# A mixture of 32 experts: fixed first blocks, paired weight loads asked for ahead, and places found before the shared expert

## The chip, the cores and the metric

The kernel runs on one core of a Trainium2 chip, as one program for a decoder of four layers. The metric is the time of one execution on the device in microseconds (us); the profiler takes one execution, and its span runs from the first to the last instruction.

## The reference, cut to what matters

Each of four layers adds a self-attention, a cross-attention and a feed-forward part to x (1024 tokens of 128 numbers). The change concerns the feed-forward part of the first layer, a mixture of experts with one choice per token and one expert that all tokens share:

```python
# H = 128, I = 256, E = 32; 1024 tokens
x = hidden_states.reshape(-1, h)
shared_out = _swiglu(x, shared_gate_w, shared_up_w, shared_down_w)
logits = x @ gate_w
topk_ids = jnp.argmax(logits, axis=-1)
topk_val = jnp.max(logits, axis=-1)
xs = x * jax.nn.sigmoid(topk_val)[:, None]
tokens_per_expert = jnp.zeros((E,), jnp.int32).at[topk_ids].add(1)
order = jnp.argsort(topk_ids)
g = ragged_dot(xs[order], routed_gate_w, tokens_per_expert)
u = ragged_dot(xs[order], routed_up_w, tokens_per_expert)
d = ragged_dot(silu(g) * u, routed_down_w, tokens_per_expert)
return shared_out + d[argsort(order)]     # _swiglu: silu(x @ gw) * (x @ uw) @ dw
```

The input of the mixture is the layer norm of x, and its result is added to x. The expert weights are one array of 33 entries, `packed`, entry 0 the shared expert, of 128 x 768 numbers each (384 KB).

## The kernel before

The program is written by engine: for each of SyncE (SP), GpSimd (POOL), VectorE, ScalarE and TensorE there is one stream of instructions that goes through the twelve parts of the decoder in order. Semaphores, wrapped in `Count` objects made by `counter`, order them: `sem.at(use, n)` is the value that a counter has after n events in its use number `use`. A stream runs strictly in its order, so an instruction that waits holds up all that stand behind it on its engine. SyncE issues nearly all transfers, on one queue.

**The first mixture (m = 0)** sorts the tokens by expert into 39 blocks of 128 rows (`blocks[0]` = 8 + 31, enough for any distribution), in `scr_x` in memory, which is filled with zero rows before. VectorE's `choose_vector` finds each token's expert. TensorE's ranking product (L1715) counts, for each token, the tokens of each expert up to it. `place_vector` finds from that how many blocks each expert needs, which expert block b belongs to (`expert_of`, event `placed` 1) and each token's row (`place`, event `placed` 2). POOL then writes the 1024 scaled tokens to their rows with eight scatters (L2044). `map_vector` turns rows back to tokens, for the way home.

The shared expert runs on TensorE between these steps: `shared_up_tensor` four times, `shared_down_tensor` once, with VectorE's multiplications `shared_vector` 0 and 1 ahead of `place_vector` and 2 and 3 behind it.

**The blocks** run in `tensor`, `scalar` and `vector`, in a loop over b from 0 to 38. Tokens come in groups of four blocks (`gb` = 4): `x_sync(g)` on SyncE loads group g from `scr_x` (256 KB, L1642) into a ring of eight blocks, and `turn_tensor(g)` transposes it on TensorE (L1783). For each block, `up_tensor` makes the two first products (L1797 and L1799, four matmuls that the trace shows as eight), ScalarE and VectorE make silu(g) * u, and `down_tensor` the second product (L1810). POOL scatters the block's result to `scr_y` (L2055). TensorE's loop is

```python
for b in range(self.nb):
    g = b // self.gb
    if b == 0:
        self.turn_tensor(pe, 0)
    if b % self.gb == self.gb // 2 and g + 1 < self.ng:
        self.turn_tensor(pe, g + 1)
    self.up_tensor(pe, b)
    if b:
        self.down_tensor(pe, b - 1)
```

so group g + 1 is turned ahead of block 4 g + 2. The weights of a block come into a ring of five slots (`WS`, `wslot`) in SyncE's `sync`: for each b from b = 4 on it waits until the last user of the slot (block b - 5; at b = 4 the shared expert) has made its second product, reads the block's expert into a register (`value_load`, L1669) and issues the load (L1670); at b = 0 it waits for the scatters and issues the token loads of groups 0 and 1, and at every b divisible by four after that the load of group b / 4 + 1.

**Before the mixture** stands the cross-attention (part n = 1). Its SyncE stream `maxima_sync` goes through 16 groups g of scores; from g = 12 on it also asks for inputs that later parts need (`late_inputs`), at the end of g = 15 it waits for them (L869) and writes the zero rows to `scr_x` and `scr_h`. The scores read the buffers `qs` (its lower half) and `ks`; the event `b_mm` counts the scores. After it, VectorE makes masks from the late inputs (L3255).

Of the kernel before, what the change touches and what calls it, by code (L numbers as in the profile page):

```python
# [79 lines left out]
def program(nc, a, ctx):  # L80
# [272 lines left out]
    class Attention:  # L353
# [497 lines left out]
        def maxima_sync(self, sp):  # L851
# [3 lines left out]
            for g in range(G):  # L855
# [11 lines left out]
                if self.n == 1 and g == G - 1:  # L867
                    sp.wait_ge(loaded, LOADED)
                    sp.dma_start(scr_x.rearrange("(p k) d -> p (k d)", p=P), w[:, 0:SLOTS]).then_inc(written, 16)  # L869
                    sp.dma_start(scr_h[0:1, :], w[0:1, 0:D]).then_inc(written, 16)  # L870
# [690 lines left out]
    m3 = range(3)  # L1561
    sh = [4 * m["shared"] for m in MOES]
# [6 lines left out]
    h_spill = counter("h_spill", [0, 4, 0], 16)  # L1569
# [8 lines left out]
    loads = [[(n + m["shared"] + WS - 1 - i) // WS for n, m in zip(blocks, MOES)] for i in range(WS)]  # L1578
    kept = [2 * len([g for g in range(LG - PR, LG) if g % 3 == i]) for i in range(WS)]
    w_in = [counter(f"w_in{i}", [n[0], n[1] + more, n[2]], 16) for i, (n, more) in enumerate(zip(loads, kept))]  # L1580
    scr_kv = nc.dram_tensor("scr_kv", [PR // 2, P, 4 * S2], F32, kind="Internal").ap()
# [21 lines left out]
    class Mixture:  # L1603
# [17 lines left out]
        def weights(self, r):  # L1621

            w, n = wslot[r % WS], self.width
            if self.relu:
                return w[:, 0:n], None, w[:, n:2 * n], w[:, 2 * n:2 * n + self.c]
            return w[:, 0:n], w[:, n:2 * n], w[:, 2 * n:3 * n], None

# [21 lines left out]
        def sync(self, sp):  # L1649
# [14 lines left out]
            sp.wait_ge(placed.sem, placed.at(m, 1))  # L1664
            for b in range(self.nb):
                r = b + self.shared
                if r >= WS:
                    sp.wait_ge(down_mm.sem, down_mm.at(m, self.sh // 2 + b - WS + 1))
                expert = sp.value_load(expert_of[b:b + 1, 0:1], min_val=0, max_val=self.e - 1 + self.shared)  # L1669
                sp.dma_start(wslot[r % WS][:, 0:n], self.packed[bass.ds(expert, 1), :, :].rearrange("o p n -> p (o n)")  # L1670
                             ).then_inc(w_in[r % WS].sem, 16)
                if self.sorted:
                    if b == self.early:
                        sp.wait_ge(sorted_out.sem, sorted_out.at(m, self.choices * NT))
                        self.x_sync(sp, 0)
                    if b == self.early or b > self.early and b % self.gb == 0 and b // self.gb + 1 < self.ng:
                        self.x_sync(sp, b // self.gb + 1)
# [72 lines left out]
        def shared_up_tensor(self, pe, k):  # L1750

            m = self.m
            gate, up, _, _ = self.weights(0)
            c, cols = k % 2, hT[:, k // 2 * 512:k // 2 * 512 + 512]
            if k >= 2:
                pe.wait_ge(hid_sb.sem, hid_sb.at(m, k - 1))
            pe.matmul(bank(k % 2), gate[:, c * P:(c + 1) * P], cols, start=True, stop=True)
            pe.matmul(bank(2 + k % 2), up[:, c * P:(c + 1) * P], cols, start=True, stop=True).then_inc(up_mm.sem, 1)

        def shared_down_tensor(self, pe):  # L1760
            m = self.m
            last = self.weights(0)[2]
# [23 lines left out]
        def up_tensor(self, pe, b):  # L1786
            m, k = self.m, self.sh + b
            r = b + self.shared
            gate, up, _, _ = self.weights(r)
            pe.wait_ge(w_in[r % WS].sem, w_in[r % WS].at(m, r // WS + 1))  # L1790
# [11 lines left out]
        def down_tensor(self, pe, b):  # L1802
            m, last = self.m, self.weights(b + self.shared)[2]
# [18 lines left out]
        def scalar(self, act):  # L1822
# [16 lines left out]
            for b in range(self.nb):  # L1839
# [6 lines left out]
                if self.relu:  # L1846
                    if b >= 2:
                        act.wait_ge(down_mm.sem, down_mm.at(m, self.sh // 2 + b - 1))
                    bias = self.weights(b + self.shared)[3]
# [44 lines left out]
        def place_vector(self, dve):  # L1894
# [6 lines left out]
            if self.choices == 1:  # L1901
# [8 lines left out]
            do(dve.tensor_scalar(need, need, ROUND, ROUND, ALU.add, ALU.subtract))  # L1910
            do(dve.memset(ones, 1.0))
# [5 lines left out]
            do(dve.scalar_tensor_tensor(out=L, in0=off.unsqueeze(1).to_broadcast([P, NT, e]), scalar=float(P),  # L1917
                                        in1=bank(6, 0, NT * 32).rearrange("p (t e) -> p t e", e=32)[:, :, 0:e],
                                        op0=ALU.mult, op1=ALU.add))
# [62 lines left out]
        def vector(self, dve):  # L1982
            m = self.m
            self.choose_vector(dve)
            if self.shared:
                self.shared_vector(dve, 0)
                self.shared_vector(dve, 1)
            self.place_vector(dve)
            xf = x[:, :, :].rearrange("p t d -> p (t d)")
            if self.shared:  # L1990
                self.shared_vector(dve, 2)
                self.shared_vector(dve, 3)
                dve.wait_ge(down_mm.sem, down_mm.at(m, 2))
                dve.tensor_tensor(xf, xf, ps[:, 4:6, :].rearrange("p b n -> p (b n)"), ALU.add).then_inc(mixed.sem, 1)
                self.map_vector(dve)
# [79 lines left out]
    g_ctx = counter("g_ctx", [1], 16)  # L2075
# [16 lines left out]
    class Gathered:  # L2092
# [23 lines left out]
        def context_tensor(self, pe):  # L2116
            pe.wait_ge(g_ctx.sem, 16)
# [134 lines left out]
    l_in = counter("l_in", [2], 16)  # L2252
# [20 lines left out]
    class Linear:  # L2273
# [141 lines left out]
        def vector(self, dve):  # L2415
            do = lambda ins: link(dve, dchain, ins)
            dve.wait_ge(l_in.sem, l_in.at(0, 2))
# [89 lines left out]
    c_in = counter("c_in", [6], 16)  # L2507
# [14 lines left out]
    class Latents:  # L2522
# [81 lines left out]
        def tensor(self, pe):  # L2604
# [6 lines left out]
            pe.wait_ge(c_in.sem, c_in.at(0, 6))  # L2611
# [85 lines left out]
        def early_turn_tensor(self, pe):  # L2697
# [5 lines left out]
            pe.wait_ge(c_in.sem, c_in.at(0, 6))  # L2703
# [109 lines left out]
        def context_vector(self, dve, half, step):  # L2813
# [3 lines left out]
            if step == 0:  # L2817
                dve.wait_ge(c_in.sem, c_in.at(0, 6))
# [84 lines left out]
    f_in = counter("f_in", [2], 16)  # L2903
# [9 lines left out]
    class Ternary:  # L2913
# [123 lines left out]
        def weights_vector(self, dve):  # L3037

            dve.wait_ge(f_in.sem, f_in.at(0, 2))
# [144 lines left out]
    def _(sp):  # L3184
# [10 lines left out]
        for s in range(N_SUB_RUN):  # L3195
            if s in subs:
                if not subs[s].prev:
                    subs[s].stack_sync(sp)
                subs[s].maxima_sync(sp)
            elif s in mixtures:  # L3200
# [272 lines left out]
```

## Time and profile before

| | before |
|---|---|
| time, median of 3 runs | 1403.6 us |
| the runs | 1397.66, 1403.6 and 3434.42 us |
| span of the profiled execution | 1397.9 us |
| TensorE busy | 1154.4 us, 83% of the span |
| VectorE busy | 888.4 us, 64% |
| ScalarE busy | 712.3 us, 51% |
| GpSimd busy | 273.4 us, 20% |
| moved by DMA | 122.46 MB, 88 GB/s on average |
| granted TensorE clock | 0.908 of full speed on average |

The profile tells the span of its own execution alone, so that the span stands for its time. The shares are averages over twelve parts with different limits, and what a change in one part does is read from the rows of that part.

### The profile page before, as it was taken

The numbers are of one execution on the slowest core, as the hardware profiler recorded it, in microseconds if no ns is written. First come the engines' busy times: TensorE is split into PE (matmuls) and PEld (weight loads), VectorE is DVE, ScalarE is ACT, GpSimd is POOL, SyncE is SP. The second block draws the span as 40 slices with busy tenths as digits, with TensorE's granted clock in tenths as the row PEclk, the third lists the DMA queues.
The fourth block names the chain that finished last, engine by engine and source line by source line (L and its number), as shares of the span: only waits on it lengthen the run. The fifth ranks groups of instructions, "written<-read, shape, count | busy, mean of one in ns | idle before, by whom it ended". The sixth has DMA issues, their size and how long they took to land.

```text
span 1397.9 us, 26573 instructions
## 1 busy us (share of the span) xinstructions
PE 1154.4 (83%) x9407; PEld 715.2 (51%) x9412; DVE 888.4 (64%) x2331; ACT 712.3 (51%) x1456; POOL 273.4 (20%) x558
## 2 busy tenths in 40 slices
PE   4889997686596399768999999999953968989994
PEld 2334344684243299555666666666643942333332
DVE  5767984334577444686676766777751166777866
ACT  3665883222452022514665665676731625656674
POOL 2522221453010256200000000000004414212220
PEclk9788999898798699989999999999985977999998
DMA  7431243684602467400000000011124825221200
GB/s 183 99 72 42 67 130 124 216 287 145 155 2 98 153 232 250 156 1 1 1 1 1 1 1 1 1 39 46 39 60 134 304 89 134 58 54 52 54 9 15
DMA packets 91620, 122.46 MB, mean 88 GB/s; under 512 B 11329, under 2 KB 69390, under 8 KB 90510
## 3 DMA queue, kind: packets, MB, share of 16 engines
q1 hardware_dynamic: 87266, 112.11, 26.4%
q0 software_dynamic: 4224, 8.66, 1.9%
q8 instruction: 77, 1.26, 0.4%
q14 instruction: 53, 0.43, 0.1%
HBM read 89.73 MB, written 30.02 MB: 86 GB/s over the span
## 4 chain that ended last, share of the span: by engine, by line
PE 62%; DVE 13%; DMA 8%; issue 5%; ACT 5%; POOL 3%; SPq 3%; DVEq 0%; ACTq 0%; POOLq 0%
PE ps L2644 7%; PE ps L2651 7%; PE ps L1168 7%; PE ps L2659 6%; PE ps L918 4%; PE ps L1797 3%; PE ps L927 3%; PE ps L1810 3%; PE ps L2733 2%; PE ps L2740 2%; PE ps L1080 2%; DMA wring<-in_L_ffn_w 2%; PE ps L1799 2%; PE ps L1203 2%; POOL scr_x L2044 2%
## 5 line engine op out<-in xcount | busy, mean ns | idle before, releaser
L1168 PE MATMUL ps<-probs,vaug 128*32 128x256 f32 (+1 forms) x1792 | 145.8, 401 | 12.4 <-ACT probs L1132 8.0
L2851 DVE CUSTOM_DVE_ANT_0 wring<-ps,probs 128x768 f32<-128x768 f32 x128 | 122.6, 958 | 46.2 <-PE ps L2644 45.5
L2810 ACT COPY qs<-ps 128x768 f32<-128x768 f32 x128 | 102.3, 800 | 90.4 <-PE ps L2651 90.4
L1123 ACT ACTIVATE probs<-ps 128x512 f32<-128x512 f32 x192 | 104.2, 595 | 62.6 <-PE ps L968 62.4
L273 POOL TENSOR_TENSOR rstd<-veps,mhalf 128x4 f32<-128x4 f32 (+2 forms) x28 | 26.5, 948 | 536.2 <-DVE veps L241 501.0
L1000 DVE TENSOR_REDUCE mx<-ps 128x2 f32<-128x1024 f32 (+1 forms) x96 | 115.5, 1220 | 20.2 <-PE ps L918 19.5
L1127 ACT ACTIVATE probs<-ps 128x512 f32<-128x512 f32 x192 | 104.8, 594 | 40.6 <-PE ps L1080 39.5
L2791 ACT ACTIVATE wring<-wring,r 128x768 f32<-128x768 f32 x128 | 120.8, 944 | 3.9 <-DVE r L2854 3.9
L2651 PE MATMUL ps<-ident,wring 128*128 128x128 f32 x768 | 110.2, 280 | 3.3 <-DVE wring L2895 3.2
L2651 PEld LDWEIGHTS ps<-ident,wring 128*128 128x128 f32 x768 | 83.4, 141 | 41.9 <-issue 35.3
L2055 POOL DMA_INDIRECT scr_y<-probs x85 | 82.1, 966 | 98.6 <-DVE probs L2009 93.3
L2644 PE MATMUL ps<-probs 64*128 64x512 f32 (+1 forms) x512 | 100.5, 511 | 1.1 <-DVE r L2851 1.1
L988 DVE CUSTOM_DVE_ANT_0 wring<-ps,m3x 128x512 f32<-128x512 f32 x128 | 83.2, 688 | 15.8 <-PE ps L918 8.7
L2659 PE MATMUL ps<-qs,ks 128*64 128x256 f32 x768 | 90.0, 384 | 0.0
L918 PE MATMUL ps<-ks,qs 49*128 49x256 bf16 (+1 forms) x512 | 81.0, 354 | 10.1 <-DMA ks<-scr_first 4.2
L2002 DVE TENSOR_TENSOR probs<-gated,ps 128x256 f32<-128x256 f32 (+1 forms) x62 | 32.2, 520 | 88.6 <-ACT gated L1857 46.8
L1797 PE MATMUL ps<-probs,wring 128*128 128x128 f32 x428 | 79.7, 293 | 8.1 <-DMA wring<-in_L_ffn_w 5.9
L2895 DVE TENSOR_SCALAR wring<-wring,r 128x768 f32<-128x768 f32 x128 | 79.5, 621 | 4.5
L1857 ACT ACTIVATE gated<-ps 128x256 f32<-128x256 f32 (+1 forms) x62 | 28.7, 463 | 87.4 <-PE ps L1799 87.4
L1797 PEld LDWEIGHTS ps<-probs,wring 128*128 128x128 f32 x428 | 63.8, 202 | 13.1 <-DMA wring<-in_L_ffn_w 9.7
L2644 PEld LDWEIGHTS ps<-probs 64*128 64x128 f32 x512 | 44.6, 187 | 47.5 <-issue 40.9
L1168 PEld LDWEIGHTS ps<-probs,vaug 128*32 128x32 f32 x1792 | 37.2, 110 | 60.8 <-issue 56.7
(366 smaller groups left out, 2337.7 us busy)
## 6 DMA issues: line engine op xcount, KB each, us to landing
wring<-in_L_ffn_w SPq DMA_DIRECT2D x19, 768.0 KB, 6.7
wring<-in_L_ffn_w SPq DMA_DIRECT2D x32, 384.0 KB, 4.2
wring<-in_L_ffn_w SPq DMA_DIRECT2D x19, 514.0 KB, 5.1
probs<-scr_x SPq DMA_DIRECT2D x14, 256.0 KB, 4.3
qs<-scr_q SPq DMA_DIRECT2D x18, 192.0 KB
qs<-scr_qx SPq DMA_DIRECT2D x16, 192.0 KB
probs<-in_L_ffn_w SPq DMA_DIRECT2D x8, 384.0 KB
probs<-in_L_ffn_w SPq DMA_DIRECT2D x4, 768.0 KB
```

The lines of the kernel that those rows point to most:

```text
L918: ins = pe.matmul(bank(at[r], i * self.keys, (i + 1) * self.keys), self.qv(s, c, r, ROWS_A, t * P, (t + 1) * P), self.kv(s, c, r, ROWS_A), ...
L1000: dve.tensor_reduce(out, src, AX.X, ALU.max, negate=True).then_inc(a_max.sem, 1)
L1123: act.activation(probs[:, s % 2, 2 * c + r, kt0 * S:(kt0 + 2) * S], bank(self.banks(3, k)[r]), ACT.Exp).then_inc(p_exp.sem, 1)
L1127: act.activation(probs[:, s % 2, 2 * c + r, kt0 * S:(kt0 + 2) * S], bank(4 + k % 2), ACT.Exp).then_inc(p_exp.sem, 1)
L1168: ins = pe.matmul(ps[32 * j:32 * j + 32, self.av_bank(s), q0:S], vaug[:, s % 2, kt, j, :], probs[:, s % 2, j, at:at + S - q0], start=(kt = ...
L1797: ins = pe.matmul(bank(k % 2)[:, at], gate[:, at], cols, start=True, stop=True)
L2644: ins = pe.matmul(bank(2 * j + lo // 512, 0, hi - lo), self.qT[rows, g % 2, k * P:(k + 1) * P], self.kT[rows, g % 3, lo:hi], start=True, s ...
L2651: ins = pe.transpose(self.buffer("turn", i, t * P, t * P + P), self.sc[:, i % 4, t * P:(t + 1) * P], ident[:, :])
L2659: ins = pe.matmul(self.buffer("sum", i, 0, S)[HW * j:HW * j + HW, :], self.v[:, i % 3, t, j * HW:(j + 1) * HW], self.pT[:, i % 2, j, t, :] ...
L2791: act.activation(self.sc[:, i % 4, :], self.sc[:, i % 4, :], ACT.Exp, bias=self.neg[:, i % 4:i % 4 + 1], accum_out=self.tot[:, i % 4:i % 4 ...
L2810: act.copy(self.pT[:, g % 2, j, :, k * P:(k + 1) * P], self.buffer("turn", i, 0, KV).rearrange("p (t n) -> p t n", n=P)).then_inc(self.out ...
L2851: dve.tensor_tensor_reduce(self.sc[:, s, :], src, self.maskb[:, u // (2 * PR), :], 1.0, -3.0e38, ALU.add, ALU.max, self.top[:, s:s + 1]).t ...
```

## The change

Block e, for e from 0 to 31, holds the first 128 tokens of expert e, whatever the others get; the seven blocks 32 to 38 hold what experts have over 128 tokens. `place_vector` therefore subtracts one block from each expert's need, finds the experts of the seven extra blocks alone, and computes a token's block from whether its rank is over 128 (three new instructions and a changed one, beside the subtraction).

The weights of blocks 0 to 31 are then known without any register: they are loaded in pairs, two experts (768 KB) in one transfer, into ten lanes (`lanes`): one slot of the ring, and parts of `qs` and `ks`. Lanes 0 to 2 are asked for by the cross-attention's SyncE stream at g = 15 after `late_inputs`, lanes 3 to 9 after its end, behind a wait for the last scores (`ahead_sync`). The others are asked for in `first_sync`, which takes the place of the loop in `sync` for this mixture. The extra blocks' weights come one by one, with the register.

On VectorE, `place_vector` follows `choose_vector` at once, then all four `shared_vector`, then `map_vector`, and then the addition of the shared expert's result to x. The lanes use counters that belonged to single later parts (`g_ctx`, `l_in`, `c_in`, `f_in`, `h_spill`); those parts count in use 1 now. The two other mixtures keep their loops.

```diff
@@ maxima_sync
                 if self.n == 1 and g == G - 1:
+                    for p in range(3):
+                        mixtures[2].lane_sync(sp, p)
                     sp.wait_ge(loaded, LOADED)
                     sp.dma_start(scr_x.rearrange("(p k) d -> p (k d)", p=P), w[:, 0:SLOTS]).then_inc(written, 16)
@@ program
+    W0 = 3 * 256
+    FIRST = MOES[0]["experts"]
+    LANES = 10
+    pairs0 = FIRST // 2 + -(-(blocks[0] - FIRST) // 2)
+    lanes = [wring[:, 1, :], *(qsf0[:, 4480 + i * 2 * W0:4480 + (i + 1) * 2 * W0] for i in range(2)),
+             *(ksf0[:, i * 2 * W0:(i + 1) * 2 * W0] for i in range(5)), *(qsf0[:, i * 2 * W0:(i + 1) * 2 * W0] for i in range(2))]
...
@@ Mixture
+        def landed(self, b):
+            if not self.shared:
+                return w_in[b % WS].sem, w_in[b % WS].at(self.m, b // WS + 1)
+            p = b // 2
+            lane = p % LANES
+            count = p // LANES + (1 if p < FIRST // 2 else b % 2 + 1)
+            return pair_in[lane].sem, pair_in[lane].at(0, count + (lane == LANES - 1))
+
+        def lane_sync(self, sp, p):
+            sp.dma_start(lanes[p % LANES].rearrange("p (o n) -> p o n", o=2),
+                         self.packed[1 + 2 * p:3 + 2 * p].rearrange("o p n -> p o n")).then_inc(pair_in[p % LANES].sem, 16)
+
+        def ahead_sync(self, sp):
+            sp.wait_ge(b_mm.sem, b_mm.at(1, G * units[1]))
+            for p in range(3, LANES):
+                self.lane_sync(sp, p)
+
+        def first_sync(self, sp):
+            m = self.m
+            sp.wait_ge(sorted_out.sem, sorted_out.at(m, self.choices * NT))
+            self.x_sync(sp, 0)
+            sp.wait_ge(placed.sem, placed.at(m, 1))
+            for b in range(self.nb):
+                if b % self.gb == 0 and b // self.gb + 1 < self.ng:
+                    self.x_sync(sp, b // self.gb + 1)
+                p = LANES + b // 2
+                if b % 2 == 0 or p >= pairs0:
+                    continue
+                sp.wait_ge(down_mm.sem, down_mm.at(m, self.sh // 2 + b + 1))
+                if p < FIRST // 2:
+                    self.lane_sync(sp, p)
+                    continue
+                for i in range(min(2, self.nb - 2 * p)):
+                    extra = 2 * p + i - FIRST
+                    expert = sp.value_load(expert_of[extra:extra + 1, 0:1], min_val=0, max_val=self.e - 1 + self.shared)
+                    sp.dma_start(lanes[p % LANES][:, i * W0:(i + 1) * W0],
+                                 self.packed[bass.ds(expert, 1), :, :].rearrange("o p n -> p (o n)")
+                                 ).then_inc(pair_in[p % LANES].sem, 16)
@@ sync
-            sp.wait_ge(placed.sem, placed.at(m, 1))
-            for b in range(self.nb):
-                r = b + self.shared
-                if r >= WS:
-                    sp.wait_ge(down_mm.sem, down_mm.at(m, self.sh // 2 + b - WS + 1))
-                expert = sp.value_load(expert_of[b:b + 1, 0:1], min_val=0, max_val=self.e - 1 + self.shared)
-                sp.dma_start(wslot[r % WS][:, 0:n], self.packed[bass.ds(expert, 1), :, :].rearrange("o p n -> p (o n)")
-                             ).then_inc(w_in[r % WS].sem, 16)
+            if self.shared:
+                self.first_sync(sp)
+            else:
+                sp.wait_ge(placed.sem, placed.at(m, 1))
...
@@ up_tensor
-            r = b + self.shared
-            gate, up, _, _ = self.weights(r)
-            pe.wait_ge(w_in[r % WS].sem, w_in[r % WS].at(m, r // WS + 1))
+            gate, up, _, _ = self.weights(b)
+            pe.wait_ge(*self.landed(b))
             pe.wait_ge(x_T.sem, x_T.at(m, b // self.gb + 1))
@@ place_vector
             do(dve.tensor_scalar(need, need, ROUND, ROUND, ALU.add, ALU.subtract))
+            if self.shared:
+                do(dve.tensor_scalar(need, need, 1.0, 0.0, ALU.subtract, ALU.max))
...
+            if self.shared:
+                extra, block = small(5)[:, 0:e], r1[:, :, 0:e]
+                do(dve.scalar_tensor_tensor(out=extra, in0=off, scalar=-1.0, in1=down[:, 0:e], op0=ALU.add, op1=ALU.add))
+                do(dve.scalar_tensor_tensor(out=block, in0=rank, scalar=float(P), in1=extra.unsqueeze(1).to_broadcast([P, NT, e]),
+                                            op0=ALU.is_gt, op1=ALU.mult))
+                do(dve.tensor_tensor(block, block, down[:, 33:33 + e].unsqueeze(1).to_broadcast([P, NT, e]), ALU.add))
+                do(dve.scalar_tensor_tensor(out=L, in0=block, scalar=float(P), in1=rank, op0=ALU.mult, op1=ALU.add))
@@ vector
             self.choose_vector(dve)
-            if self.shared:
-                self.shared_vector(dve, 0)
-                self.shared_vector(dve, 1)
             self.place_vector(dve)
             xf = x[:, :, :].rearrange("p t d -> p (t d)")
             if self.shared:
-                self.shared_vector(dve, 2)
-                self.shared_vector(dve, 3)
+                for k in range(self.sh):
+                    self.shared_vector(dve, k)
+                self.map_vector(dve)
                 dve.wait_ge(down_mm.sem, down_mm.at(m, 2))
                 dve.tensor_tensor(xf, xf, ps[:, 4:6, :].rearrange("p b n -> p (b n)"), ALU.add).then_inc(mixed.sem, 1)
-                self.map_vector(dve)
@@ block.sync
                 subs[s].maxima_sync(sp)
+                if s == 1:
+                    mixtures[2].ahead_sync(sp)
```

## Rows read from the trace of the kernel before

**Rows 1.** The page: the span, and from section 6 one DMA issue group.
```profile
span 1397.9 us, 26573 instructions
...
wring<-in_L_ffn_w SPq DMA_DIRECT2D x19, 768.0 KB, 6.7
```

**Rows 2.** Windows, the blocks: us, busy PE, PEld, DVE, ACT, POOL, clock, DMA, GB/s.
```profile
255.30:326.00 70.70, 63.34 (x502) 59.54 (x503) 23.50 (x75) 20.42 (x49) 34.90 (x37) 0.96 0.86 276
```

**Rows 3.** Timeline of TensorE: start, us, instruction; the blocks' first and last.
```profile
255.33 1.11 PE L1783 MATMUL ps<-ident,probs 128*128 128x128 f32 x4 [5.33 <-DMA probs<-scr_x]
...
326.85 0.71 PE L1810 MATMUL ps<-probs 128*128 128x128 f32 x4 [0.55 <-DVE probs L2002]
```

**Rows 4.** Timeline of TensorE, second products and a turn, no weight late.
```profile
264.13 0.61 PE L1810 MATMUL ps<-wring,probs 128*128 128x128 f32 x4
...
265.47 0.61 PE L1810 MATMUL ps<-probs 128*128 128x128 f32 x4
...
267.25 0.60 PE L1783 MATMUL ps<-ident,probs 128*128 128x128 f32 x4
```

**Rows 5.** Timeline ahead of the mixture: SyncE's zero rows, VectorE's first mask.
```profile
217.01 0.34 SPq L869 DMA_DIRECT2D scr_x<-w  x1
...
221.66 0.68 DVE L3255 TENSOR_SCALAR m3a<-m3a_raw 128x1024 bf16<-128x1024 uint8 x1
```

**Rows 6.** Timeline of VectorE, ScalarE and POOL from the choice to the scatters.
```profile
231.06 0.29 DVE L1884 CAST probs<-comb 128x256 bf16<-128x256 f32 x1
231.39 0.21 ACT L1829 ACTIVATE rcol<-rcol 128x8 f32<-128x8 f32 x1 [3.79 <-DVE probs L1884]
...
234.74 0.17 DVE L1904 TENSOR_SCALAR rcol<-rcol 128x8 f32<-128x8 f32 x1
...
237.87 0.42 DVE L1917 SCALAR_TENSOR_TENSOR lg<-probs,ps 128x256 f32<-128x256 f32 x1
...
239.24 0.17 DVE L1924 TENSOR_SCALAR place<-probs 128x8 int32<-128x8 f32 x1
...
250.26 0.20 DVE L1967 SCALAR_TENSOR_TENSOR probs<-ps,probs 128x39 int32<-128x39 f32 x1
250.37 0.96 POOL L2044 DMA_INDIRECT scr_x<-h,place  x1 [0.30 <-issue]
```

**Rows 7.** The chain of waits: start, us, what; SyncE behind a second product.
```profile
279.17 0.46 PE ps L1810 x4
...
280.37 0.34 SPq L1670
...
280.75 0.47 SPq L1642
```

**Rows 8.** Lines L1670, then L1642, from 280.3 to 281.3: issue (ns), landing (us).
```profile
L1670 SPq DMA_DIRECT2D wring<-in_L_ffn_w x1: 338/338/338, 280.4 to 280.4; - x1
...
DMA to landing us min/median/max: 6.1/6.1/6.1
...
L1642 SPq DMA_DIRECT2D probs<-scr_x x1: 472/472/472, 280.7 to 280.7; - x1
...
DMA to landing us min/median/max: 6.4/6.4/6.4
```

**Rows 9.** Line L1670, 235 to 245: 384 KB into an empty queue.
```profile
DMA to landing us min/median/max: 3.1/3.1/3.1
```

**Rows 10.** Line L1670, 512 to 520: 768 KB loads of the second mixture.
```profile
DMA to landing us min/median/max: 5.0/5.3/5.7
```

**Rows 11.** Line L1642, 250 to 256: token loads into an empty queue.
```profile
DMA to landing us min/median/max: 2.7/2.8/3.0
```

**Rows 12.** Windows, columns as in rows 2, around an idle stretch and the blocks' start.
```profile
18.90:22.00 3.10, 0.04 (x1) 0.00 (x0) 2.91 (x5) 2.20 (x4) 0.00 (x0) 1.00 0.76 268
22.00:25.20 3.20, 3.16 (x4) 1.30 (x5) 2.62 (x4) 0.96 (x2) 1.62 (x1) 0.56 0.09 30
...
255.30:260.70 5.40, 4.65 (x20) 4.28 (x21) 0.42 (x1) 0.97 (x2) 0.00 (x0) 0.50 0.95 307
```

## Prediction before the change was run

> **What bounds the kernel now.** I read the page for the span, then the windows over the first mixture, then the timeline and the chain of waits inside it, because the change touches nothing else but some loads just ahead of it. The span is 1397.9 us [rows 1]. The mixture's 39 blocks fill the stretch from the first transposes at 255.33 to the end of the last product at 326.85 + 0.71 = 327.56, which is 72.2 us [rows 3]. In nearly all of it TensorE is busy for 63.3 of 70.7 us, and the DMA engines for 86% of the time at 276 GB/s [rows 2]. So two things lie close together there: a TensorE that is almost full, and loads of 384 KB for every block that almost fill the DMA engines. What TensorE takes by itself is read where no weight is late: the second products (L1810) of two neighbouring blocks start 1.34 us apart (264.13, 265.47), and one more turn of four blocks adds 267.25 - 266.81 = 0.44 us (266.81 is 265.47 + 1.34) [rows 4]. With no wait after block 3 the stretch would be: 265.47 + 0.61 - 255.33 = 10.75 to the end of block 3's second product (the first blocks run at the lower clock), 34 blocks by 1.34 = 45.6 and a last product 0.45, eight turns by 0.44 = 3.5, about 1.0 for the last block's way through ScalarE and VectorE (0.55 idle and its 0.71 stand in the row): **61.3 us**. The waits for weights are thus worth 72.2 - 61.3 = **10.9 us**, and nothing that keeps weights ready can give back more inside the blocks.
>
> **Part 1, loads in the cross-attention.** Three pairs (2.4 MB) are asked for behind the late masks and ahead of the zero rows for scr_x (2.5 MB, now asked for at 217.01), seven (5.5 MB) behind those [rows 5]. At 276 GB/s [rows 2] the three pairs and the zero rows take 4.9 MB / 276 = 18 us from about 213, so the zero rows land near 231; POOL waits for them before its first scatter, which can't start before the places are known at about 238. The cover is 7 us; if it were gone, the mixture would start late by what is missing. The masks that VectorE reads at 221.66 [rows 5] stand ahead in the queue. The last of the seven lands near 251 and is used at block 18. The queue's wait for the end of the scores has only the mixture's own requests behind it. Cost: nothing; bounds 0 and +2 us, should the scatters share the DMA engines with the last pairs (part 2 waits for the last of them only).
>
> **Part 2, places first.** VectorE now has the choice at 231.06 + 0.29, but takes up the places at 234.74 (L1904), because two multiplications of the shared expert stand between; ScalarE's exponential is there at 231.39 + 0.21 = 231.60 [rows 6]. So the places can start at 231.65, 3.1 us sooner. Four instructions are added: two of 128x256 elements like L1917, 0.42 each and 0.45 with the gap to the next, and two of 128x32, for which I take 0.25, between L1904's 0.17 and L1917's 0.42 [rows 6]. That is 2 x 0.45 + 2 x 0.25 = 1.4, and the places come 3.1 - 1.4 = 1.7 us sooner, at 237.7 for 239.4. The eight scatters, the last issued at 250.37 [rows 6], and the first load of tokens move along: blocks begin at 253.6. What pays for it is the shared expert: its multiplications start at about 237.75 for 233.5, 4.2 us later, and TensorE's second half of it with them. The map of slots, which ends at 250.26 + 0.20 [rows 6] and which the first turn waits for, moves ahead of the addition into x (which saves 1.3) and back by those 4.2, less the little that it waited for: some 250 to 253, still not the last to come. Gain **1.7 us**; bounds 0 (map as late as the tokens) and 2.5.
>
> **Part 3, weights in pairs.** Twenty blocks have their weights before they begin, and pair 10 is asked for when block 1 is done, 18 blocks ahead of its use. All of the 10.9 us of waits goes. But the loads of tokens (x_sync) sit in the same SyncE program, and here is the price. Before, group 3's load at b = 8 stood behind a wait for block 3. Now first_sync waits at every odd b for block b itself, issues that pair, and only then comes to x_sync at b + 1. So group 2's tokens are asked for after block 3 is done, group 3's after block 7, groups 4, 5 and 6 after blocks 11, 15 and 19; and turn_tensor wants them at blocks 6, 10, 14, 18 and 22. TensorE runs its stream in order, and between the end of block 3's second product and that turn it has only one more block, 1.34 us. From block 20 on nothing waits, and groups 7 to 9 are asked for in good time. Five turns stall.
>
> How long? The pair's issue needs no register load, so it starts about 0.05 after the second product's end; with one, the issue came at 280.37 after 279.17 + 0.46, 0.74 later, and the tokens' 0.38 behind it [rows 7]. The tokens land behind the weights asked for just before them: 280.4 + 6.1 = 286.5 and 280.7 + 6.4 = 287.1, 0.6 to 0.7 apart [rows 8]. A pair of 768 KB: 384 KB into an empty queue took 3.1 us [rows 9], and 384 KB more at 276 GB/s adds 1.4, so 4.5; loads of 768 KB of the second mixture took 5.0 to 5.7 in a good stretch [rows 10] and 6.7 in the median [rows 1]. The pairs come 2.7 us apart here and overlap a little; I take 4.7, near the first. Then 0.05 + 4.7 + 0.7 - 1.34 = **4.1 us** for each of groups 2, 3 and 4. Group 5's tokens stand behind two single loads with register loads: 0.75 + 1.1 + 3.6 + 0.7 - 1.34 = 4.8. Group 6's stand behind one: 0.75 + 3.6 + 0.7 - 1.34 = 3.7 (3.6 for 384 KB, between 3.1 and the 6.1 of rows 8). Sum **20.8 us**. The low end is tokens not held behind the pair: 0.45 + 2.7 as in an empty queue [rows 11] - 1.34 = 1.8 each, 9.0. The high end takes 6.7 for a pair and 6.1 for a single load: 3 x 6.1 + 7.3 + 6.2 = 31.8.
>
> The Trainium skill puts a transfer at 2.0 us plus its bytes at 436 GB/s (page "DMA: Bandwidth & Descriptors", section "Anatomy of one DMA — SWDGE (gpsimd) path", measured on GpSimd's queue). By that a pair would take, as an estimate, 3.8 us, and three stalls would be 0.9 shorter each, 2.7 in all; the 3.1 of rows 9, where it gives 2.9, speaks for slightly more than it says.
>
> **The clock after a stall.** When TensorE idled for 3.1 us before 22.0, the granted clock was 1.00 in the wait and 0.56 in the 3.2 us that followed, though it was busy for nearly all of them; after the 5.33 us idle before the blocks it was 0.50 for 5.4 us [rows 12, 3]. These are the levels of 2.4 and 1.2 GHz. Stalls of 4 us lie between the two, so each should be followed by some 3.5 us at half speed, which loses 1.75: five make **8.8 us**. Ends: 0 (stalls of 1.8 us might leave it) and 5 x 2.7 = 13.5.
>
> **Sum.** The blocks take 61.3 + 20.8 + 8.8 = 90.9 us for 72.2, which is +18.7; less 1.7 makes +17.0, and the span 1414.9. The 1397.9 lie beside the fastest run shown (1397.66) and 5.7 under the median of 1403.6 (the third run, 3434, tells nothing). I put 2 us for that on top: **1417 us**. The ends are 61.3 + 9.0 - 72.2 - 1.7 = -3.6 and 61.3 + 31.8 + 13.5 - 72.2 = +34.4 without part 2's gain.
>
> **Rivals.** First, it is not slower: the tokens' packets are taken up while the pair is still moving, so that a stall is 1.8 us and the clock stands. That gives -3.6 and 1396. It decides at (10.9 + 1.7) / 5 = 2.5 us per stall, clock included, that is, with tokens landing 3.9 us after a block's end. For it speaks 2.7 us in an empty queue; against it that tokens landed behind the weights, in order of their issue [rows 8, 11]. Chance 0.13.
>
> Second, the clock does not come back between the stalls: blocks 6 to 21 all at half speed lose 16 x 1.34 + 4 x 0.44 = 23.2 in place of four of the five falls (7.0), and the block beside each transfer then hides 1.34 more of it, four times 5.4 less: 17.0 + 23.2 - 7.0 - 5.4 = +27.8, 1428. For it: at the start of the blocks the low clock lasted 5.4 us, and there are only some six us of work between stalls; against it the 3.2 us after 22.0. The Trainium skill describes just such a kernel, whose short bursts of matmuls between DMA waits each start at the lower clock again (page "TensorE: Matmul & The Clock Gate", section "HAM oscillation — how this bites in real kernels"); rows 12 agree with its direction for one wait, and no run here shows a row of them yet. Chance 0.12.
>
> Third, the loads ahead are not ahead: the zero rows land after 238 and hold the scatters, or the masks come late. With the queue at the 200 GB/s that small packets might leave it, 4.9 MB take 25 us, which is just covered; beyond that it costs some 5 us more, 1422. Chance 0.05.
>
> **How the numbers follow.** The forecast has 0.70. The range runs from 1399, which leaves out the first rival, to 1434, which takes in the second and most of the dear end of the unknown stalls; about 2 in 10 stay outside. 2% of 1403.6 is 28 us, about what a measurement of this kernel can tell from no change. Faster by that would need more than all the idle time of the stretch: 0.01. Slower by that takes the forecast's upper tail (0.08) and half of the second rival (0.06): 0.14. Within 2%: 0.85.
>
> **What would show it.** In the timeline of after, TensorE's transposes ahead of blocks 6, 10, 14, 18 and 22 come after some 4 us of idle time that the load of tokens ends, with the granted clock at 0.5 behind each; no first product waits for weights; the places come at 237.7; from block 22 the blocks run 1.34 us apart; the stretch takes about 91 us. Gaps under 2.5 us, or none, prove me wrong on the order of landing; a stretch over 98 us on the clock; a first turn after 256 on part 1 or 2.

## The result, and the profile after

The changed kernel takes 1423.8 us in the median of four runs (1421.79 to 1427.34), for 1400.63 of the kernel before; the ratio is **1.0165, with a 95% interval of 1.0141 to 1.019**. The profiled execution's span is 1423.0 us for 1397.9 [rows 1], +25.1. The forecast was 1417 in a range of 1399 to 1434: slower, but by less than 2%.

The page, and the windows over the blocks with the columns of [rows 2]:

```profile
span 1423.0 us, 26406 instructions
```
```profile
251.80:349.30 97.50, 71.21 (x507) 69.51 (x507) 24.21 (x77) 20.69 (x49) 35.57 (x38) 0.81 0.39 124
```

The stretch that took 72.2 us now takes 97.5. TensorE, almost full before, idles for over a quarter of it, the granted clock is 0.81 for 0.96, and the DMA engines, which were at 86%, are at 39% [rows 2]. Neither TensorE nor the DMA engines bound the blocks any more; an order of waiting does. The timeline of TensorE shows which. These are its turns of token groups 0 to 7 and its last product, with the idle time ahead of each:

```profile
251.76 1.12 PE L1849 MATMUL ps<-ident,probs 128*128 128x128 f32 x4 [3.72 <-DMA probs<-scr_x]
257.81 0.60 PE L1849 MATMUL ps<-ident,probs 128*128 128x128 f32 x4
267.85 1.12 PE L1849 MATMUL ps<-ident,probs 128*128 128x128 f32 x4 [4.08 <-DMA probs<-scr_x]
280.76 1.11 PE L1849 MATMUL ps<-ident,probs 128*128 128x128 f32 x4 [5.29 <-DMA probs<-scr_x]
293.10 1.12 PE L1849 MATMUL ps<-ident,probs 128*128 128x128 f32 x4 [4.36 <-DMA probs<-scr_x]
307.65 1.11 PE L1849 MATMUL ps<-ident,probs 128*128 128x128 f32 x4 [5.95 <-DMA probs<-scr_x]
321.12 1.11 PE L1849 MATMUL ps<-ident,probs 128*128 128x128 f32 x4 [5.29 <-DMA probs<-scr_x]
329.21 0.60 PE L1849 MATMUL ps<-ident,probs 128*128 128x128 f32 x4
...
348.55 0.71 PE L1875 MATMUL ps<-qs,probs 128*128 128x128 f32 x4 [0.55 <-DVE probs L2075]
```

Group 1's turn comes without a wait, groups 2 to 6 each wait 4 to 6 us for a load of tokens, together 25.0 us, and group 7 no more. Each stalled turn takes 1.1 us for 0.6, which is already the low clock. No wait for weights is left: in the list of waits the only DMA that TensorE waits for in the blocks is the tokens' (the total includes the first turn's 3.7):

```profile
PE ps L1849 <- DMA probs<-scr_x: 28.7, 6, 5.9
```

What the stalls of groups 2 and 5 waited for, by line: L1660 is a pair and L1706 the tokens of group 2, L1688 the single load ahead of the tokens of group 5 (the issue itself in ns, then issue to landing in us):

```profile
L1660 SPq DMA_DIRECT2D qs<-in_L_ffn_w x1: 373/373/373, 262.5 to 262.5; - x1
...
DMA to landing us min/median/max: 4.6/4.6/4.6
...
L1706 SPq DMA_DIRECT2D probs<-scr_x x1: 469/469/469, 262.9 to 262.9; - x1
...
DMA to landing us min/median/max: 4.9/4.9/4.9
...
L1688 SPq DMA_DIRECT2D ks<-in_L_ffn_w x1: 338/338/338, 302.2 to 302.2; - x1
...
DMA to landing us min/median/max: 4.7/4.7/4.7
```

The tokens of group 2 land at 262.9 + 4.9 = 267.8, 0.7 behind the pair (262.5 + 4.6 = 267.1), and TensorE's turn starts at 267.85. The windows of the stall and of what follows it show the clock:

```profile
263.80:267.80 4.00, 0.00 (x0) 0.00 (x0) 0.62 (x2) 0.00 (x0) 1.51 (x2) 1.00 0.88 308
267.85:271.20 3.35, 3.35 (x16) 3.35 (x17) 0.00 (x1) 0.97 (x2) 0.00 (x0) 0.50 0.01 2
271.20:275.50 4.30, 4.27 (x38) 4.08 (x37) 1.86 (x6) 1.15 (x3) 2.30 (x3) 0.99 0.68 204
```

The clock is 1.00 while TensorE waits, 0.50 in the 3.35 us after, in which TensorE is busy throughout, and then back: 16 instructions in the slow 3.35 us, 38 in the 4.30 that follow.

Places first did what it should. VectorE's choice, its first step towards the places, and the places:

```profile
229.89 0.29 DVE L1949 CAST probs<-comb 128x256 bf16<-128x256 f32 x1
...
230.45 0.17 DVE L1969 TENSOR_SCALAR rcol<-rcol 128x8 f32<-128x8 f32 x1 [0.27 <-ACT rcol L1894]
...
236.31 0.17 DVE L2000 TENSOR_SCALAR place<-probs 128x8 int32<-128x8 f32 x1
```

From the choice to the places it is 6.42 us for 239.24 - 231.06 = 8.18 [rows 6], 1.76 less. The first turn comes 251.76 - 229.89 = 21.9 us behind the choice for 24.3, 2.4 less.

So the 25.1 us of the span are +25.3 in the blocks, -2.4 between the choice and the blocks, and +2.2 elsewhere: the choice itself came 1.2 earlier (the change adds only loads ahead of it), and what follows the blocks took 3.4 longer (1423.0 - 349.26 = 1073.7 for 1397.9 - 327.56 = 1070.3). That last part scatters from run to run: it is 1069.8 us in one of the kernels below and 1077.2 in another, all with the same code there. A difference of a few us in the whole time is therefore read here from the stretch, not from the total.

### The profile page after: what moved, and what is told of

The parts are those of the page before. It is cut to its first block, busy times and chain, and to the rows that moved or that the text cites. A ratio compares the mean times of both kernels' runs of the same rounds, so it can differ in the third digit from the quotient of the medians.

```text
span 1423.0 us, 26406 instructions
## 1 busy us (share of the span) xinstructions
PE 1169.2 (82%) x9412; PEld 726.8 (51%) x9412; DVE 889.3 (62%) x2335; ACT 711.7 (50%) x1456; POOL 272.5 (19%) x558
## 4 chain that ended last, share of the span: by engine, by line
PE 63%; DVE 13%; DMA 7%; issue 5%; ACT 5%; POOL 3%; SPq 3%; DVEq 0%; ACTq 0%; POOLq 0%
PE ps L2714 7%; PE ps L2721 7%; PE ps L1170 6%; PE ps L2729 6%; PE ps L1862 4%; PE ps L920 4%; PE ps L1875 3%; PE ps L929 3%; PE ps L1864 2%; PE ps L2803 2%; PE ps L2810 2%; DMA probs<-scr_x 2%; PE ps L1082 2%; PE ps L1205 2%; POOL scr_x L2117 2%
## 5 line engine op out<-in xcount | busy, mean ns | idle before, releaser
L1170 PE MATMUL ps<-probs,vaug 128*32 128x256 f32 (+1 forms) x1792 | 145.5, 400 | 12.1 <-ACT probs L1134 7.9
L2729 PEld LDWEIGHTS ps<-qs,ks 128*64 128x64 f32 x768 | 52.3, 137 | 28.4 <-issue 5.2
L1849 PE MATMUL ps<-ident,probs 128*128 128x128 f32 x85 | 18.0, 333 | 57.4 <-DMA probs<-scr_x 49.5
```

The source lines that it names most:

```text
L1170: ins = pe.matmul(ps[32 * j:32 * j + 32, self.av_bank(s), q0:S], vaug[:, s % 2, kt, j, :], probs[:, s % 2, j, at:at + S - q0], start=(kt = ...
L2729: ins = pe.matmul(self.buffer("sum", i, 0, S)[HW * j:HW * j + HW, :], self.v[:, i % 3, t, j * HW:(j + 1) * HW], self.pT[:, i % 2, j, t, :] ...
```

## The experiments

Two theories stood against each other. **Mine:** the tokens are asked for too late, by the order of SyncE's program; two thirds of a stall is the pair that the tokens land behind, and each stall costs the clock as well. **Rivals:** the transfers themselves are the bound; the landing order doesn't matter; the low clock costs nothing because the next transfer sets the period. The runs with tokens asked for early, with tokens ahead of the pair, with filled stalls and with ten pairs at the mixture's start shared one chip; the old order on VectorE, five pairs ahead and 16 fill matmuls a second; 12 fill matmuls and the repeat of early tokens a third. All ratios are to the kernel before, run on the same chip; lengths of stretches come from one profiled execution each.

### Tokens asked for as soon as their ring slots are free

```diff
-                if b % self.gb == 0 and b // self.gb + 1 < self.ng:
-                    self.x_sync(sp, b // self.gb + 1)
+                for g in range(1, self.ng):
+                    if b == (0 if g == 1 else max(1, 4 * g - 9)):
+                        self.x_sync(sp, g)
```

> My theory (tokens are asked for too late, in SyncE's order): each token load from group 2 on is asked for as soon as its ring slots are free, four blocks sooner, so no turn stalls and the clock stays up. The blocks take 61 to 64 us for 97.5 with the change, the execution about 1388 us, ratio to before about 0.990. Rival (the transfers, not the order, are the bound: pairs, tokens and results make 2.1 MB per four blocks of 5.8 us, 360 GB/s where 276 to 310 were reached): the tokens land late wherever they are asked for, gaps of 2 to 4 us stay ahead of blocks 10 to 22, blocks over 75 us, 1400 us or more.

Measured: 1385.66 us, ratio 0.9884 (0.9859 to 0.9909). The turns of groups 0, 3, 4 and 5, the last product, and two rows of the list of waits:

```profile
253.54 1.11 PE L1850 MATMUL ps<-ident,probs 128*128 128x128 f32 x4 [3.81 <-DMA probs<-scr_x]
...
271.12 0.60 PE L1850 MATMUL ps<-ident,probs 128*128 128x128 f32 x4
276.91 0.60 PE L1850 MATMUL ps<-ident,probs 128*128 128x128 f32 x4
283.29 0.60 PE L1850 MATMUL ps<-ident,probs 128*128 128x128 f32 x4
...
315.21 0.71 PE L1876 MATMUL ps<-qs,probs 128*128 128x128 f32 x4 [0.55 <-DVE probs L2076]
```
```profile
DVE probs L2083 <- DMA scr_y<-probs: 6.6, 8, 1.4
...
PE ps L1876 <- DVE probs L2076: 1.3, 4, 0.6
```

No turn waits for its tokens any more but the first. Most turns come 5.8 us apart, four blocks of 1.34 and a turn of 0.44; those of groups 5, 6 and 7 come 6.3 to 6.4 behind the one before, 1.6 us more in all, where second products waited for VectorE, and VectorE for earlier results to be written to `scr_y`. The blocks take 315.92 - 253.54 = 62.4 us. Three changed lines in SyncE's program are worth 35 us there against the change. The loads are no quicker: the tokens of groups 3 to 6 land 4.4 to 6.4 us behind their request, those of groups 2 to 6 in the change 4.9 to 6.1. They are only asked for sooner. The rival of full DMA engines falls: the same bytes went through in two thirds of the time.

### Tokens ahead of the pair, behind the same wait

```diff
                 sp.wait_ge(down_mm.sem, down_mm.at(m, self.sh // 2 + b + 1))
+                if b % self.gb == self.gb - 1:
+                    self.x_sync(sp, (b + 1) // self.gb + 1)
                 if p < FIRST // 2:
                     self.lane_sync(sp, p)
```

(where these loads, groups 2 to 6, were asked for in the change, they are left out)

> The tokens of groups 2 to 6 are asked for behind the same wait for a block's end, but ahead of that wait's pair. My theory (about two thirds of each stall is the pair that the tokens land behind, the rest is the late request itself): gaps of 1.4 to 2.5 us remain at the five turns for 4.1 to 6.0, the clock falls less often, about 1405 us, ratio about 1.004. Rival (a transfer in flight does not hold a later one; the stall is the latency of the tokens' own load): gaps stay at 4 to 6 us, 1422 us.

Measured: 1403.64 us, ratio 1.002 (0.9993 to 1.0048), blocks 78.0 us. The five turns:

```profile
264.23 0.66 PE L1851 MATMUL ps<-ident,probs 128*128 128x128 f32 x4 [1.89 <-DMA probs<-scr_x]
272.14 0.66 PE L1851 MATMUL ps<-ident,probs 128*128 128x128 f32 x4 [1.89 <-DMA probs<-scr_x]
281.58 0.66 PE L1851 MATMUL ps<-ident,probs 128*128 128x128 f32 x4 [1.80 <-DMA probs<-scr_x]
290.91 1.12 PE L1851 MATMUL ps<-ident,probs 128*128 128x128 f32 x4 [3.31 <-DMA probs<-scr_x]
301.03 1.12 PE L1851 MATMUL ps<-ident,probs 128*128 128x128 f32 x4 [2.78 <-DMA probs<-scr_x]
```

The stalls fall from 25.0 to 11.7 us, so more than half of them was the place behind the weights; the rest is the late request. The last two gaps are longer than the expected 2.5: there the tokens were asked for within 2 us behind two single loads, and landed 4.6 and 4.0 us after their request, for 3.1 to 3.2 in the first three. What is in flight ahead matters, and that rival falls too. The clock behind the short stalls is a result by itself; windows behind the first and the second of 1.89 us:

```profile
264.20:268.20 4.00, 3.97 (x36) 3.97 (x37) 1.17 (x4) 1.35 (x3) 1.03 (x2) 1.00 0.66 205
272.10:276.10 4.00, 3.96 (x23) 3.96 (x24) 0.66 (x2) 0.97 (x2) 0.73 (x2) 0.64 0.57 188
```

After the same idle time the clock stood once and fell once; after the 1.80 of the third turn it stood.

### The stalls filled with matmuls

```diff
+            if m == 0 and 2 <= g <= 6:
+                pe.wait_ge(x_T.sem, x_T.at(m, g))
+                for _ in range(16):
+                    pe.matmul(bank(6 + g % 2), identb[:, :], m3a[:, 0, :], start=True, stop=True)
             if self.sorted:
                 pe.wait_ge(x_in[g % 2].sem, x_in[g % 2].at(m, g // 2 + 1))
```

> The change, with 16 bf16 matmuls of 128x512 (3.5 us at full clock; results not used) ahead of the wait in the five turns that stall. My theory of the clock: the granted clock stays at 1.00 behind the stalls, which gives back about 2 us each, about 1414 us, ratio 1.009, with the tokens landing as late as before. Rival (the half clock behind a stall costs nothing, because the next tokens' transfer sets the period): no difference, 1424 us.

Measured: 1412.82 us, ratio 1.0088 (1.0056 to 1.0121), blocks 335.55 - 247.04 = 88.5 us. The tokens come as late as in the change: fill matmuls and idle time in the five turns make 18.1 + 7.5 = 25.6 us, for 25.0 of idle time there. Yet 9.0 us are back. Windows behind two of the turns, the second behind the one place where 2.6 us stayed idle:

```profile
264.00:268.00 4.00, 3.99 (x36) 3.99 (x37) 1.20 (x4) 1.35 (x3) 0.96 (x1) 1.00 0.20 33
...
296.90:300.90 4.00, 3.97 (x22) 3.97 (x23) 0.71 (x2) 0.97 (x2) 0.19 (x1) 0.59 0.01 2
```

Where TensorE had been kept busy, with 0.8 to 1.6 us of idle time left, the clock stayed at 1.00; so it was at four of the five turns. The low clock after a wait costs real time, and the rival falls.

### The old order on VectorE

The early-token kernel, with `shared_vector` 0 and 1 ahead of `place_vector`, 2 and 3 behind it, and the map behind the addition, as in the kernel before.

> As the run with early tokens, with VectorE's old order (two shared multiplications ahead of the places, the map behind the addition to x). My theory (placing first is worth 1.7 us, 2.4 us by the trace of the change): from the choice to the first turn 24 us for 21.9, about 1388 us for 1385.7, hardly more than the runs scatter. Rival (the later shared expert and map cost as much as it gains): the same stretch from the choice to the first turn in both.

Measured: 1392.98 us, ratio 0.9929 (0.9902 to 0.9956). Choice, places, first turn:

```profile
228.49 0.29 DVE L1950 CAST probs<-comb 128x256 bf16<-128x256 f32 x1
...
238.02 0.17 DVE L2001 TENSOR_SCALAR place<-probs 128x8 int32<-128x8 f32 x1
...
253.73 1.12 PE L1850 MATMUL ps<-ident,probs 128*128 128x128 f32 x4 [5.32 <-DMA probs<-scr_x]
```

The places come 9.53 us behind the choice, for 6.42 with the new order and 8.18 before: the order gains 3.11 and the four added instructions cost 1.35. The first turn is 25.2 behind the choice, for the 24 expected, and for 21.9 with early tokens alone. The repeat of that kernel (below) has 22.7, so the part is worth 2.5 to 3.3 us at the first turn. The blocks are 0.9 us shorter here, 61.5 for 62.4, so that less is left at their end. The totals differ by more, but by no more than the runs scatter.

### No pair asked for in the cross-attention

Two kernels with early tokens. In the first, all ten pairs are asked for at the mixture's start:

```diff
+            self.x_sync(sp, 1)
+            for p in range(LANES):
+                if p in (3, 6):
+                    self.x_sync(sp, 1 + p // 3)
+                self.lane_sync(sp, p)
             sp.wait_ge(placed.sem, placed.at(m, 1))
```

> As the run with early tokens, but no pair is asked for in the cross-attention: the ten first ones are asked for behind the first two token loads, tokens of groups 2 and 3 between them. My theory (pairs of 768 KB arrive every 2.8 us at 276 GB/s, two blocks and half a turn's share take 2.9): the first block waits about 4 us for its pair and some of the next for 0 to 1 us, together 4 to 10 us more than with the loads ahead, about 1395 us. Rival (asking ahead is worth as much as the waits of before, 10.9 us and more): 1400 us or over; other rival (it is worth nothing): the same time as with early tokens.

Measured: 1400.16 us, ratio 0.9991 (0.997 to 1.0011), blocks 71.8 us. From its list of waits:

```profile
PE ps L1853 <- DMA probs<-scr_x: 9.7, 2, 5.8
...
PE ps L1866 <- DMA wring<-in_L_ffn_w: 4.0, 1, 4.0
```

The first block waits 4.0 us for its pair, as expected; the other 5.8 are the turn of group 4, whose tokens were asked for behind the queue of pairs and landed 14.9 us later: the change's mistake once more in another place, and mine. The total fits the rival's number, but the list of waits does not fit its reason: it is not the weights. So a second kernel asks for five pairs ahead of use and no more (`p = 5 + b // 2`, five pairs at the start):

> As the run with early tokens, but no pair is asked for in the cross-attention, and in the mixture always five pairs ahead of use, so that no long queue stands before the tokens. My theory (what asking ahead is worth is the first block's wait for its pair, 4 us in the run without it, and the fall of the clock; the stall at block 14 in that run was its tokens behind a long queue): only the first block waits, 4 us, blocks 66 to 69 us, about 1391 us. Rival (pairs asked for in time can't keep up at 2.7 us for two blocks): waits for weights of 0.5 to 1 us at many blocks, 72 us or more, 1397 us or more.

Measured: 1395.03 us, ratio 0.9944 (0.9924 to 0.9964), blocks 66.4 us. Its only wait for weights:

```profile
260.11 0.80 PE L1866 MATMUL ps<-probs,wring 128*128 128x128 f32 x2 [3.95 <-DMA wring<-in_L_ffn_w]
```

Asking ahead in the cross-attention is thus worth the first block's 4 us, and 66.4 - 62.4 = 4.0 says the same. The total is 4 us over the 1391 expected, the blocks are as expected. The rest of what the waits for weights had cost is saved in the mixture itself; how much of it comes from the pairs, how much from doing without a register and how much from the early request was not tried one by one.

### The first turn's wait filled

The early-token kernel with 16, then 12 of the fill matmuls ahead of the first turn's wait; the second beside the early-token kernel once more.

> As the run with early tokens, with 16 bf16 matmuls of 128x512 (3.5 us at full clock; results not used) ahead of the first turn's wait for tokens. My theory (the low clock of the first two blocks comes from the 3.8 us of idle time ahead of them): the clock is 1.00 from the first block on, blocks 60 us for 62.4, about 1383 us. Rival (the fill delays the first turn, or the clock falls all the same): the same time or 1 to 3 us more.

> As e6, with 12 fill matmuls for 16, so that they end before the tokens land. My theory: first turn 21.9 us behind the choice as without fill, blocks 60.2 us, 2 us less than e1_again, ratio lower by 0.0015, at the edge of what the runs tell. Rival (the fill is given back: later parts lose what the blocks gain): the same time as e1_again or more.

> The kernel with early tokens once more, beside the next run on one chip. My theory: ratio to before 0.988 to 0.991, blocks 62.4 us. Rival (its first result was a lucky draw of what the later parts take): ratio 0.993 or more with the same blocks.

Measured: 1391.59 us (ratio 0.9916, 0.9883 to 0.995) with 16, 1390.65 (0.9906, 0.9883 to 0.9928) with 12, and 1393.14 (0.9918, 0.9892 to 0.9945) for early tokens alone. Windows at the start of the blocks, the change first and then the kernel with 16 fill matmuls:

```profile
251.76:257.20 5.44, 4.72 (x21) 4.35 (x22) 0.42 (x1) 0.97 (x2) 0.00 (x0) 0.50 0.06 17
```
```profile
253.70:259.20 5.50, 4.74 (x39) 4.32 (x38) 1.04 (x3) 1.95 (x5) 0.27 (x1) 1.00 0.16 48
```

With 16 the clock is up from the first block and the blocks take 60.2 us for 62.4, but the fill ends late: the first turn comes 253.73 - 250.20 = 3.5 us behind the request for its tokens, for 253.54 - 250.80 = 2.7 without fill. The total is 1391.59 where I expected 1383. With 12 only 1.25 us stay idle ahead of the turn, but the clock falls all the same, a little later, and the blocks take 62.0 for the 60.2 expected. A gain of 1 to 2 us is inside the scatter, and whether the fill is worth its instructions stays open. The repeated kernel's stretch is 62.7 us for 62.4, but its total is 7 us above its first result, and its ratio lies between what I and the rival expected: its six runs lie between 1384.84 and 1394.44. Its two intervals overlap from 0.9892 to 0.9909, so early tokens are about 1% faster than before, and more can't be said.

## Why the prediction held, and where it was off

The direction, the five stalls, their places and the fall of the clock behind each came as forecast. The size did not: the span grew by 25.1 us for the 17.0 of the sum, with the stalls and the clock both put too low.

**The stalls: the right cause, five of them, at the forecast turns.** Late tokens behind the pair were shown by moving the request (all five gone) and by swapping the order (more than half gone). The sum was too low: 25.0 us for 20.8. Groups 2 and 4, at 4.08 and 4.36, are close to the 4.1 forecast; group 3 took 5.29. What was mis-sized is the single load ahead of groups 5 and 6, "3.6 for 384 KB": the last one before the tokens took 4.7 and 5.0 us, and those two stalls were 5.95 and 5.29 for 4.8 and 3.7. That is 2.7 of the 4.2 missed. Both loads were asked for with another still in flight; the two of the seven single loads that had none in flight ahead took 3.2 us, the five others 3.7 to 5.0. Group 3's tokens landed 6.1 us behind their request, for 4.9 and 5.2 of groups 2 and 4; why is not shown.

The Trainium skill's line for a transfer (page "DMA: Bandwidth & Descriptors", section "Anatomy of one DMA — SWDGE (gpsimd) path") gave 3.8 us for a pair as an estimate. The trace has 4.6 for the pair above, and the measurement decides: the rows that I took, 4.7, were nearer.

**The clock: right in kind, too low in size.** I put some 3.5 us at half speed behind each stall, 8.8 us in all. The stretches from each stalled turn to the next wait (the last one to the next turn), all with TensorE busy, give more:

```profile
267.85:275.47 7.62, 7.62 (x52) 7.43 (x52) 1.86 (x6) 2.12 (x5) 2.27 (x3) 0.78 0.38 114
280.76:288.74 7.98, 7.97 (x52) 7.79 (x52) 1.90 (x6) 2.12 (x5) 2.28 (x3) 0.74 0.35 112
293.10:301.70 8.60, 8.60 (x52) 8.41 (x52) 1.90 (x6) 2.12 (x5) 2.27 (x3) 0.68 0.30 90
307.65:315.83 8.18, 8.17 (x52) 7.98 (x52) 1.95 (x6) 2.12 (x5) 2.28 (x3) 0.72 0.30 96
321.12:329.21 8.09, 8.09 (x52) 8.09 (x53) 1.90 (x6) 1.98 (x5) 2.10 (x3) 0.71 0.14 45
```

Each holds one turn and four blocks, which take 5.80 us at full clock. Together they are 40.5 us for 29.0, so the low clock cost **11.5 us**, 2.3 a stall. By their mean clock the half speed lasted 3.4 to 5.5 us. Filling the stalls gave 9.0 back, at four of the five turns. The second rival, a clock that never comes back, falls with the window at 0.99 after 271.2. The Trainium skill's description of short bursts that start slow after each DMA wait (page "TensorE: Matmul & The Clock Gate", section "HAM oscillation — how this bites in real kernels") agrees here: all five stalls of 4.08 us and more were followed by 1.2 GHz.

**No waits for weights: right.** Without stalls and low clock behind them the change's blocks are 97.5 - 25.0 - 11.5 = 61.0 us, for 61.3 forecast; the 62.4 with early tokens hold 1.6 us of waits for results, which the change does not have. One reading behind the 61.3 was wrong: the 0.44 taken for a turn runs from the start of a second product to the start of the turn [rows 4], so it is that product. The value holds all the same: 5.80 - 4 x 1.34 = 0.44.

**Places first: right in size.** 1.76 us for 1.7 at the places, 2.4 at the first turn. The 0.7 more lies between the places and the last scatter, which was issued at 250.37 - 239.24 = 11.1 us behind the places before [rows 6] and 10.2 after. One late scatter takes longer than the usual 0.96 in both profiles, first before, then after:

```profile
248.23 1.84 POOL L2044 DMA_INDIRECT scr_x<-h,place  x1 [0.31 <-issue]
```
```profile
246.55 1.26 POOL L2117 DMA_INDIRECT scr_x<-h,place  x1 [0.30 <-issue]
```

So the last scatter ends 12.1 us behind the places before and 11.5 after, which is 0.6 of the 0.7. In the two executions of the early-token kernel that long scatter takes 1.21 and 1.84, so this part scatters by itself and is not credited to the change.

**Loads in the cross-attention: no cost there**, as forecast, and the masks and zero rows were in time. They moved faster than the 276 GB/s that I took, 409 GB/s from 213 to 238, so the last pair landed at 227.5 + 14.3 = 241.8 where I had 251. The first rival (tokens not held behind the pair) is refuted by the landings and by the swapped order. Its price for a stall, 1.8 us, is what the swap came to in its first three stalls.

**The sum** was 6.6 us too low in the blocks: 4.2 for the stalls, 2.7 for the clock, less 0.3 for the stretch without waits. The span, 1423.0, is 8.1 over the 1414.9: these 6.6, less 0.7 gained ahead of the blocks beyond the forecast, and 2.2 elsewhere.

## What to carry to other kernels

When a wait moves, list everything that stands behind it in the same engine's program: here a load of 256 KB that nobody meant to touch was put behind a later wait and a longer transfer, and that cost more than all the waits that the change removed. Ask for a block's data when its buffer becomes free, not when the program next comes past; but a small load asked for behind a long queue of large ones is late as well, as the ten pairs at the mixture's start showed. Here a lower busy share of the DMA engines together with a slower stretch was the mark of such an order; the first place to look is which transfer ends the idle time, and then when it was asked for.

## What was not expected of the hardware

SyncE itself was held while it issued. Two of the first pairs' issues and the seven later ones, from the timeline of the changed kernel, then the fifth of the seven by itself:

```profile
211.81 1.15 SPq L1660 DMA_DIRECT2D qs<-in_L_ffn_w  x2
...
216.42 9.44 SPq L1660 DMA_DIRECT2D ks<-in_L_ffn_w  x5
225.90 3.34 SPq L1660 DMA_DIRECT2D qs<-in_L_ffn_w  x2
```
```profile
218.51 7.35 SPq L1660 DMA_DIRECT2D ks<-in_L_ffn_w  x1
```

The two took 1.15 us together, the next five 9.44, of which the fifth alone is 7.35, and the last two 3.34, with no wait in the program between the seven. When the fifth was issued, eight pairs and the zero rows, 8.8 MB, had been asked for since 211.26. What held it is not shown. It cost nothing here: the next load in SyncE's program waited another 19.8 us for the scatters.

And waits of 1.8 and 1.9 us were followed by the full clock twice and by the low one once, where the waits of 2.6 us and more ahead of these turns were all followed by the low one. What decides between the two was not tried; with 12 fill matmuls even 1.25 us of idle time was followed by a fall.
